# A router that reads activations: taking an expert layer's logits past its last product

## What is computed

```python
# _L0_cond2_ref: one expert per batch entry, chosen from cond_8
up = einsum('bsd,bhd->bsh', x, wu) + bu
gate = einsum('bsd,bhd->bsh', x, wg) + bg
hidden = silu(up) * gate
out = einsum('bsh,bdh->bsd', hidden, wd) + bd
# _L0_ffn_ref: 8 experts, 2 per token, at most 640 tokens each
logits = x @ Wg.T                       # x is the out above, Wg is (8, 256)
top_v, top_i = top_k(logits, 2)
pos = cumsum(one_hot(top_i), axis=0) - 1  # a token's place in its expert
exp_batches = zeros((8, 640, 256)).at[expert, pos].set(x[tok])
h = einsum('ecd,edf->ecf', exp_batches, W1); h = gelu(inp) * gate
exp_out = einsum('eci,eid->ecd', h, W2)
```

## Time and profile before

| | |
|---|---|
| three runs | 1037.69, 1039.23, 1040.01 us (median 1039.23) |
| profiled execution | 1037.52 us, span 1035.9 us |
| TensorE busy | 939.1 us, 91% of the span |
| VectorE, ScalarE, GpSimd busy | 521.2, 440.6, 283.1 us |
| chain that ended last | TensorE 70%, VectorE 16%, ScalarE 5%, DMA 3% |

### The profile page before, as it was taken

One profiled execution on the slowest core, in us unless ns is written; L12 is line 12 of the kernel. 1 busy time (PEld: TensorE's weight loads), 2 busy tenths in 40 slices (PEclk: granted clock), 3 DMA queues, 4 the chain that ended last, 5 costly groups with the idle time before them and its releaser, 6 DMA issues.

```text
span 1035.9 us, 13076 instructions
## 1 busy us (share of the span) xinstructions
PE 939.1 (91%) x4808; PEld 784.2 (76%) x4808; DVE 521.2 (50%) x1010; ACT 440.6 (43%) x831; POOL 283.1 (27%) x246
## 2 busy tenths in 40 slices
PE   3889998997759799998489999999999999999898
PEld 2667867886639699998467788888888888887686
DVE  6545353567635745554457733333333333588644
ACT  1555565433125345554234434335334343325675
POOL 8233321102035445553635003204022040000000
PEclk9899999998959999998789999999999999999999
DMA  7120000311224144324252120300303003000011
GB/s 254 31 73 21 21 1 1 148 33 70 82 56 109 43 132 149 130 52 147 65 174 60 27 107 1 122 1 1 122 1 122 1 1 122 1 1 1 1 41 41
DMA packets 21070, 66.41 MB, mean 64 GB/s; under 512 B 4432, under 2 KB 11856, under 8 KB 18704
## 3 DMA queue, kind: packets, MB, share of 16 engines
q1 hardware_dynamic: 15872, 38.82, 10.7%
q0 software_dynamic: 4416, 25.44, 8.5%
q10 hardware_dynamic: 720, 1.32, 0.3%
HBM read 54.04 MB, written 9.44 MB: 61 GB/s over the span
## 4 chain that ended last, share of the span: by engine, by line
PE 70%; DVE 16%; ACT 5%; issue 4%; DMA 3%; SPq 1%; POOL 0%; DVEq 0%; ACTq 0%; POOLq 0%
PE banks L857 15%; PE banks L859 14%; PE banks L858 14%; PE banks L1033 4%; PE banks L1031 4%; PE banks L1032 4%; PE banks L927 3%; PE banks L911 2%; PE banks L1081 1%; PE banks L1080 1%; PE banks L1067 1%; DMA expert_output<-y_rows 1%; PE banks L1068 1%; PE banks L918 1%; PE banks L881 1%
## 5 line engine op out<-in xcount | busy, mean ns | idle before, releaser
L857 PE MATMUL banks<-input_hi,mlp_hi 128*128 128x512 f32 x384 | 153.2, 399 | 1.5 <-DVE input_lo L1617 1.5
L859 PE MATMUL banks<-input_hi,mlp_lo 128*128 128x512 f32 x384 | 151.4, 394 | 0.0
L858 PE MATMUL banks<-input_lo,mlp_hi 128*128 128x512 f32 x384 | 150.9, 393 | 0.0
L1824 POOL TENSOR_TENSOR mlp_lo<-weight_stage,mlp_hi 128x768 fp32r<-128x768 f32 x40 | 74.2, 1855 | 240.1 <-ACT mlp_hi L1269 240.1
L1284 ACT CAST hidden_hi<-hidden 128x512 fp32r<-128x512 f32 x96 | 59.5, 620 | 175.6 <-DVE hidden L1627 108.0
L1633 DVE TENSOR_TENSOR hidden_lo<-hidden,hidden_hi 128x512 fp32r<-128x512 f32 x96 | 66.5, 692 | 71.5 <-ACT hidden_hi L1284 71.5
L1627 DVE SCALAR_TENSOR_TENSOR hidden<-banks,L_expert_weight,gelu 128x512 f32<-128x512 f32 x64 | 48.0, 750 | 99.4 <-PE banks L859 99.3
L1794 POOL TENSOR_TENSOR ffn_w_lo<-weight_stage,ffn_w_hi 128x512 fp32r<-128x512 f32 x48 | 62.1, 1296 | 116.6 <-ACT ffn_w_hi L1226 116.6
L857 PE MATMUL banks<-expert_in_hi,ffn_w_hi 128*128 128x320 f32 x256 | 82.8, 324 | 8.7 <-DVE hidden L1581 5.7
L857 PEld LDWEIGHTS banks<-input_hi,mlp_hi 128*128 128x128 f32 x384 | 72.5, 189 | 17.3 <-issue 1.9
L859 PEld LDWEIGHTS banks<-input_hi,mlp_lo 128*128 128x128 f32 x384 | 72.6, 189 | 16.4
(11 more groups left out here) (279 smaller groups left out, 2144.5 us busy)
## 6 DMA issues: line engine op xcount, KB each, us to landing
weight_stage<-in_packF SPq DMA_DIRECT2D x8, 1536.0 KB, 6.8
weight_stage<-in_shared SPq DMA_DIRECT2D x2, 3072.0 KB, 10.4
expert_output<-y_rows SPq DMA_DIRECT2D x40, 128.0 KB, 3.0
weight_stage<-in_cond_w SPq DMA_DIRECT2D x4, 512.0 KB, 7.9
residual<-in_xT SPq DMA_DIRECT2D x4, 512.0 KB, 13.8
first_half_swapped<-first_half SPq DMA_DIRECT2D x32, 64.0 KB, 2.0
routed_input<-x_rows SPq DMA_DIRECT2D x16, 128.0 KB, 1.7
weight_stage<-in_ffn_w SPq DMA_DIRECT2D x2, 1024.0 KB, 9.3
```

The costliest lines, as they stand in the source:

```text
L857: pe.matmul(o, wh, dh, start=(i == 0), stop=False)
L858: pe.matmul(o, wh, dl, start=False, stop=False)
L859: last = pe.matmul(o, wl, dh, start=False, stop=(i == len(terms) - 1))
L1824: pool.tensor_tensor(wDl[s][:, qs], stage[:, qs], f(wDh[s][:, qs]), ALU.subtract).then_inc(done)
```

## The change

The down weights and their bias of both experts are loaded once more by row (`down_by_row`, two indirect DMAs on GpSimd in front of `pack0`). As the last step of `split0(b)` TensorE multiplies the router through them (`wg`), and ScalarE and VectorE split the result in two parts side by side (`wg_hi`, `wg_lo`: 16 columns). A chunk's logits are then eight products of 16 columns by 512 tokens over the activations (`lgT`), biased and copied by ScalarE (`lg_row`), and turned back to token rows, with the two parts summed, by four small products (`lg`). The transposes and copies of x rows go. `down` of a chunk is issued behind all of the next chunk's `up`, its fourth tile behind `lgT`; in the last chunk the routing has no steps between, and the x rows are placed by hand inside it. The weight split starts right behind the first `up`, with `w0_lo` of the second expert on GpSimd, and the routed expert's 22 steps after it. The slot table is 40 columns by 128 rows instead of 160 by 32 repeated, and the one-hots of a chunk are three wide operations instead of 16. The router weights have memory of their own and are loaded at the start, so SyncE has no wait for the end of attention. Three tiles of the first routed expert are turned in before its first product, the other two behind it. Some semaphores are merged.

```diff
 I1 = 1024
 R = 16
 FF = 4 * D
-LOW = 32
-HIGH = CAP // LOW
-GH = G * HIGH
+GS = G * ST
+ROW = KD * H0 + KD
 QT = CH // P
 K = 2
 HT = H0 // P
...
+DELAY = 22
 
...
             act.append(("w0_hi", b, q))
-            dve.append(("w0_lo", b, q))
+            (pool if b else dve).append(("w0_lo_pool" if b else "w0_lo", b, q))
             if q < PIECES0 - 1:
                 yield
         act.append(("b0", b))
+        product("out", "wg", b)
+        act.append(("wg_hi", b))
+        dve.append(("wg_lo", b))
         yield
...
-    use("down", [(3,), (4,)])
-    use("turn2", [(5,), (6,)])
+    use("down", [(3,), (4,), (5,)])
+    use("turn2", [(6,)])
...
-            dve.append(("xrow", c, t))
-            rows_done.add(c * QT + t)
+            if c < NCH - 1:
+                dve.append(("xrow", c, t))
             yield
 
-    logits_done = set()
-
...
+
+    def logits(c):
+        product("turn2", "lgT", c)
+        act.append(("lg_row", c))
+        routing.append(route_chunk(c))
+        yield
+
+    def route_chunk(c):
+        last = c == NCH - 1
+        yield
+        yield
+        product("turn2", "lg", c)
+        dve.append(("first", c))
+        if not last:
             yield
-        logits(columns)
-        logits_done.add(c)
-        yield
-
-    def route_chunk(c):
-        while c not in logits_done:
+        dve.append(("second", c))
+        if not last:
             yield
-        for step in ("first", "second", "m16", "first_row"):
-            dve.append((step, c))
-            yield
+        dve.append(("m16", c))
+        dve.append(("first_row", c))
+        if last:
+            dve.append(("xrow", c, 0))
+        yield
+        yield
         product("turn2", "cnt", c)
         dve.append(("pos", c))
-        yield
         dve.append(("place", c))
-        yield
+        if last:
+            dve.append(("xrow", c, 1))
         dve.append(("digits", c))
-        yield
-        for k in range(K):
-            for t in range(QT):
-                dve.append(("at", c, k, t))
-            yield
-            for t in range(QT):
-                if (c, k, t) == (0, 0, 0):
-                    banks["inv", c, k, t] = (7,)
-                pe.append(("inv", c, k, t))
+        if last:
+            dve.append(("xrow", c, 2))
+        dve.append(("at", c))
+        if last:
+            dve.append(("xrow", c, 3))
+        yield
+        if not last:
+            yield from [None] * 4
+        if c == 0:
+            banks["inv", c] = (7,)
+        pe.append(("inv", c))
+        yield
...
     def all_chunks():
         yield from ups[0]
-        weights = chain([None] * 4, split0(1))
-        for c in range(NCH):
-            if c == CPB:
-                weights = split_expert(0)
-            steps = chain(some(ups[c + 1], HT + 1), down_chunk(c), ups[c + 1]) if c + 1 < NCH else chain([None] * 3, down_chunk(c))
-            yield from weave(steps, weights)
-
-    run(weave(weave(all_chunks(), chain(*[chunk_logits(c) for c in range(NCH)])), chain(*[route_chunk(c) for c in range(NCH)])))
+        yield from some(ups[1], 2)
+        yield from logits(0)
+        for c in range(1, NCH):
+            yield from ups[c]
+            behind = down_chunk(c - 1)
+            yield from some(behind, 3)
+            if c == NCH - 1:
+                use("down", [(3,), (4,), (5,), (0,), (1,), (2,)])
+            yield from logits(c)
+            yield from behind
+        yield from down_chunk(NCH - 1)
+
+    weights = chain([None] * 4, split0(1), [None] * DELAY, split_expert(0))
+    for _ in all_chunks():
+        next(weights, None)
+        routing = [g for g in routing if next(g, "ended") != "ended"]
+    while routing:
+        routing = [g for g in routing if next(g, "ended") != "ended"]
     act.append(("slots",))
...
-    def turn_in(e):
-        for j in range(ST):
+    def turn_in(e, first=0, end=ST):
+        for j in range(first, end):
             product("turn3", "xe", e, j)
             act.append(("xe_hi", e, j))
             dve.append(("xe_lo", e, j))
             yield
 
     def coming_expert(e):
-        if e:
-            yield from split_expert(e)
+        if e == 1:
+            yield from turn_in(0, FIRST_HALF, ST)
...
     gather(0)
-    run(coming_expert(0))
+    run(turn_in(0, 0, FIRST_HALF))
...
+                pe.wait_ge(*ready("w0_lo_pool" if b else "w0_lo", b, PIECES0 - 1))
...
                 dh, dl = parts(wBh[b], H0)[2], parts(wBl[b], H0)[2]
                 pe.wait_ge(*ready("hid_lo", c, HT - 1))
                 products(o[:, 0:D], [(hidH[n][:, k, ts], hidL[n][:, k, ts], dh[:, k, :], dl[:, k, :]) for k in range(HT)], done)
-            elif kind == "xt":
-                c, t = key
-                xr = xrow[(c * QT + t) % 6]
-                pe.wait_ge(*ready("xrow", c, t))
-                for k in range(KD):
-                    last = pe.transpose(o[:, k * P:(k + 1) * P], xr[:, k * P:(k + 1) * P], ident[:, :])
+            elif kind == "wg":
+                b, = key
+                pe.wait_ge(ld["wg"], 16)
+                pe.wait_ge(ld["by_row"], 16 * B)
+                for k in range(HT):
+                    for m in range(KD):
+                        pe.matmul(o[:, k * G:(k + 1) * G], by_row[b][:, m * H0 + k * P:m * H0 + (k + 1) * P], wgT[:, m, :], start=(m == 0), stop=(m == KD - 1))
+                for m in range(KD):
+                    last = pe.matmul(o[0:G, HT * G:HT * G + 1], wgT[:, m, :], by_row[b][:, KD * H0 + m:KD * H0 + m + 1], start=(m == 0), stop=(m == KD - 1))
                 last.then_inc(done)
-            elif kind == "logit":
-                c, t = key
-                xc = xcol[(c * QT + t) % 2]
-                pe.wait_ge(*ready("xcol", c, t))
-                pe.wait_ge(ld["wg"], 16)
-                for k in range(KD):
-                    last = pe.matmul(o[:, 0:G], xc[:, k, :], wgT[:, k, :], start=(k == 0), stop=(k == KD - 1))
+            elif kind == "lgT":
+                c, = key
+                pe.wait_ge(*ready("wg_lo", c // CPB))
+                pe.wait_ge(*ready("hid_lo", c, HT - 1))
+                for k in range(HT):
+                    pe.matmul(o[0:2 * G, :], wg16[c // CPB][:, k, :], hidH[c % 2][:, k, :], start=(k == 0), stop=False)
+                    last = pe.matmul(o[0:2 * G, :], wg16[c // CPB][:, k, :], hidL[c % 2][:, k, :], start=False, stop=(k == HT - 1))
+                last.then_inc(done)
+            elif kind == "lg":
+                c, = key
+                pe.wait_ge(*ready("lg_row", c))
+                for t in range(QT):
+                    last = pe.matmul(o[:, t * G:(t + 1) * G], lg16[c % 2][:, t * P:(t + 1) * P], both_parts[:, :], start=True, stop=True)
                 last.then_inc(done)
             elif kind == "cnt":
                 c, = key
@@ -972,11 +1004,12 @@
                     last = pe.matmul(o[:, QT * G:(QT + 1) * G], ones16[:, :], m[:, u, :], start=(u == 0), stop=(u == QT - 1))
                 last.then_inc(done)
             elif kind == "inv":
-                c, k, t = key
-                n = k * QT + t
-                pe.wait_ge(*ready("at", c, k, t))
-                pe.matmul(banks[:, 7, 0:GH], at_low[n][:, :], at_col[n][:, :], start=(c == 0 and n == 0),
-                          stop=(c == NCH - 1 and n == K * QT - 1)).then_inc(done)
+                c, = key
+                pe.wait_ge(*ready("at", c))
+                for n in range(K * QT):
+                    last = pe.matmul(banks[:, 7, 0:GS], at_low[c % 2][:, n, :], at_col[c % 2][:, n, :], start=(c == 0 and n == 0),
+                                     stop=(c == NCH - 1 and n == K * QT - 1))
+                last.then_inc(done)
             elif kind == "xe":
...
                 s, hs, ms = e % 2, slice(h * HALF, (h + 1) * HALF), slice(part * I0 + i * P, part * I0 + (i + 1) * P)
-                if h == 0 and i == 0 and part == 0:
-                    pe.wait_ge(*ready("xe_lo", e, ST - 1))
+                if i == 0 and part == 0:
...
-                act.wait_ge(*ready("xt", c, t))
-                act.copy(xcol[n % 2][:, :, :], bank(("xt", c, t))[:, 0:D].rearrange("p (k t) -> p k t", k=KD)).then_inc(done)
+            elif kind == "wg_hi":
+                b, = key
+                act.wait_ge(constants, CONSTS)
+                act.wait_ge(*ready("wg", b))
+                act.copy(lgb[b][0:G, :], bank(("wg", b))[0:G, HT * G:HT * G + 1])
+                act.copy(wg16[b][:, :, 0:G], bank(("wg", b))[:, 0:HT * G].rearrange("p (k g) -> p k g", g=G)).then_inc(done)
+            elif kind == "lg_row":
+                c, = key
+                if c >= 2:
+                    act.wait_ge(*ready("lg", c - 2))
+                act.wait_ge(*ready("lgT", c))
+                act.activation(lg16[c % 2][:, :], bank(("lgT", c))[0:2 * G, :], ACT.Identity, bias=lgb[c // CPB][:, 0:1]).then_inc(done)
             elif kind == "wf_hi":
                 e, q = key
...
             elif kind == "slots":
```

(54 more changed lines are left out.)

87 lines of the change are left out of this document (40 added, 47 removed).

## The result

The changed kernel takes **1029.05 us** (median of four runs, 1027.82 to 1029.48) beside 1039.62 of the kernel before (four runs): ratio 0.9898, 95% interval 0.9884 to 0.9912. It is 1.0% faster; 1028 with a range of 1015 to 1037 was predicted. Its profiled execution has a span of 1027.8 us, against 1035.9 before.

The account below looks back on a forecast made before the run. The prediction took the bound to be a chain through VectorE with TensorE work laid around it. 9.3 - 2.2 + 3.9 = 11.0 us off the profiled 1037.5 gave 1026.5, plus 1.7 for the median: 1028, range 1015 to 1037.

Parts of the forecast that it names:

- E: End of the last logits: forecast at 272.7 instead of 281.99, 9.3 us earlier, with 11.7 us of waits and low clock.
- (a): Second expert's `w0_hi` casts on ScalarE wait for weights landing at 197.9; `silu(1,0)` queues behind two, TensorE waits 0.7 us.
- (b): Count of chunk 0: `wg_lo(1)` stands before `first(0)` on VectorE and waits for ScalarE's casts; TensorE waits 2.5 us.
- (c): Chunk 1: count, place, digits and one-hots hold VectorE 4.3 us in one piece; `lgT(2)` comes 1.9 us late.
- (d): Chunk 2: same VectorE piece beside GpSimd's `wf_lo` subtractions; 0.6 us at the count, 4.2 at `lgT(3)`, about 1.8 low clock.
- One-hots: On VectorE per chunk: three wide operations take 2.3 us instead of 3.8 for 16 narrow ones; bounds 1.9 and 3.8.
- Store and tail: Last logits to first gather: 13.4 us, 2.2 more than before, as the last x row's store takes 4.0 to land.
- the second rival: Gathers run beside the fetch issued right behind the last store and take 4 us longer: 1032; chance 0.08.
- Gather to the first product: First gather to first routed expert product: three tiles needed instead of five, 8.0 us instead of 11.9, 3.9 gained.
- The first: Rival: the waits (a) to (d) are mostly covered, 9 of the 11.7 us gone: 1019; chance 0.20.
- The third: Rival: shared interfaces, twelve GpSimd subtractions each stop a VectorE operation some 1.1 us; 7 us beyond (d), 1035; chance 0.15.
- The fourth: Rival, slower than before: TensorE's clock falls to 1.2 GHz at each of five waits; 15 us of such work, 1043; chance 0.07.

Follow-up runs that it names:

- `best6`: `best5` with the splits of expert 0's weights begun four steps later (DELAY 26 instead of 22): 1020.81 us.
- `at_late`: Changed kernel with the wide one-hots of chunks 0 to 2 five steps later, behind the next chunk's last `hid_lo`: 1023.00 us.
- `best2`: Changed kernel with place, digits and one-hots of chunks 0 to 2 five steps later, and expert 2's fetch held until expert 0's gathered tiles are transposed: 1021.66 us.
- `narrow`: Changed kernel with a chunk's three wide one-hot operations made 16 narrow ones again, the 40 columns kept: 1031.44 us.
- `fetch_late`: Changed kernel with the fetch of expert 2's weights held back until expert 0's five gathered tiles are transposed and split: 1026.63 us.
- `all5`: Changed kernel with all five gathered tiles of the first expert transposed before its first product, instead of three: 1031.11 us.
- `tiles_high`: Changed kernel with its new router tiles at the top of local memory, so later buffers have the addresses of the kernel before: 1022.83 us.
- `best5`: `best2` with the router tiles also at the top of local memory: 1018.16 us.

## Why the prediction was right, step by step

The total lies inside the range and close to the forecast, but four of its terms were off by 2 us or more, and they happened to cancel.

- **E.** Forecast 86.6 us after the stage's start (272.7 from 186.08); measured 86.2. Inside, two errors cancel. The waits came to 5.1 us and the low clock to about 3.4, 8.5 together instead of 11.7; TensorE's work to 77.7 instead of 74.9 (in part `lg`, whose eight passes span 1.05 us, not 0.7).
- **(a)** 0.7 forecast, none seen: the second expert's weights were there at 195.5, not 197.9. ScalarE of the changed kernel:

```profile
195.53 1.14 ACT L1220 CAST expert_hi<-weight_stage 128x512 fp32r<-128x512 f32 x2 [1.71 <-DMA weight_stage<-in_pack,rows_of_L_cond]
```

- **(b)** 2.5 forecast, 0.83 seen. **(c)** 1.9 forecast, 0.62. The positions in the queues were right, and both estimates of when the chain would be done were one to two us too late.
- **(d)** 0.6 and 4.2 forecast, 1.39 and 2.27 seen; the low clock behind it 1.8 forecast and 1.7 seen (0.58 granted from 263.9 to 268). Both causes that it names were there: the collisions at the count (`best6`), and at `lgT(3)` the one-hots in front of the last `hid_lo` (`at_late`). The 1.45 us left there went when place and digits were moved too (`best2`); how much of it was their stretching by GpSimd and how much their own length is not shown.
- **One-hots.** 2.3 forecast, 2.07 seen. The Trainium skill, VectorE: DVE Perf Modes, The perf-mode tier table, spoke against the wide form. In `narrow` 16 narrow operations take 3.25 us and the three wide ones 2.07: the trace disagrees with the estimate, which scaled the figures of that table by the number of elements. At these widths the fixed part of an instruction decides: from start to start a 128x40 operation takes 0.21 us and a 128x128 one 0.19.
- **Store and tail.** E to the gather: 13.4 forecast, 11.3 seen. The step that failed is the landing, and it failed in the reading: of the two stores in the earlier trace rows the one of 4.0 us is the last but one (issued at 276.88, landed at 280.86). The last one, with the fetch 0.4 us behind it, had landed in 1.85 us, and with that the sum gives E + 11.3. The fetch follows again, 0.4 us behind, and the store lands in 1.71. What the fetch slows is the gather, which is the second rival's mechanism; it predicted 4 us, and `fetch_late` measures 0.5 at the first product. And "the inverse is early" was not so by the 3 us of the forecast: the cast of its table ended 0.11 us behind the landing, at E + 10.4, where the forecast had it.
- **Gather to the first product.** 8.0 forecast, 8.4 seen. `all5` prices the part at 3.5 us there, but 3.0 at the end of expert 0: the transposes of two tiles did not go, they moved. My 3.9 counted them as gained; the error is small.
- **"A gain at the first product is a gain at the end"** is the step that failed most: 6.0 of 14.05 us were given back. I had named a fetch or a store as what could take it; neither did. About 3 us are the products' pace, which buffers moved by 672 bytes changed (`tiles_high`); the rest is mostly clock.
- **The median.** I added 1.7 us, the distance of the profiled execution of the kernel before from its median. The profiled execution of the changed kernel is its median, 1029.05, and 8.5 us under that of the kernel before, not 11.0. The missing gain and the needless 1.7 nearly cancel; that is luck.
- **Rivals.** The first (waits mostly covered) was half right: 5.1 us of waits instead of 9.9. With the low clock it left 2.7 of the 11.7 us, and 8.5 were measured, nearer to the forecast. The third, GpSimd's casts of b = 1, stretched one instruction, by 0.4 us. The fourth: of the four waits before E one was followed by a fall of the clock, and one fall came without a wait.

## What to carry to other kernels

A small persistent tile added ahead of other buffers shifts all of them; when the same products run at another pace at full clock, compare the counts of products in equal stretches and put the tile elsewhere before looking for a cause in the schedule. Follow each hand-ordered VectorE queue for what stands in front of the instruction that the bottleneck waits for, and move whole blocks behind it. A wait removed by moving work is only gained when nothing queued behind the moved work holds a bank or a buffer.

## What the runs showed of the hardware

**Addresses.** The product pace of 128x512 fp32 products differs by up to 2% between placements of their operands 32 to 704 bytes apart, and the first-layer means repeat within 0.2 ns over eight kernels of one placement. Not expected, and not explained here.

**The clock.** The changed kernel runs 29 small products and then falls to half clock with no wait before it. Its TensorE: the small products, and the 4.2 us behind them:

```profile
199.57:202.50 2.93, 2.93 (x29) 1.00 0.00 0
202.50:206.70 4.20, 4.20 (x12) 0.59 0.00 0
```

`at_late` has the same order of instructions up to there, and its clock stays up (the stretch that holds the same products):

```profile
200.00:208.00 8.00, 8.00 (x51) 1.00 0.00 0
```

`best2` and `best5` differ in nothing but the place of the router tiles; the first runs at full clock from 203 to 207 us, the second at 0.62. So of one such fall, 1.7 us, no profile of a single execution can say whose it is. Differences under 2 us between the kernels above are to be read with that.

**VectorE beside GpSimd.** The small instructions that take long beside GpSimd do not run slower: they end with it. Not only those with two inputs are held (`row<-place` of `best6`, with one, took 0.92 us); small reductions and small instructions with an input from a PSUM bank took their usual 0.17 to 0.22 us beside it. The Trainium skill, SBUF — State Buffer, Terms, calls the pair of ports that the two share an exclusive lock, held for a whole instruction, so that the other fully blocks. By that rule, the trace agrees: 0.86 and 1.20 us instead of 0.19, the last ending 0.06 us behind GpSimd's.
